# Moving the output combination behind the gating of the next tile on VectorE's queue

## The chip, the cores and the metric

The kernel runs on all 8 cores of one Trainium2 chip, one batch element on each, with the same program and no exchange between them. The metric is the device time of the slowest core, in microseconds (us). Each core has TensorE (matmuls), VectorE, ScalarE, GpSimd, and SyncE, whose queue issues most of the DMAs here. Each engine takes its instructions in the order in which they were written for it.

## What is computed

The reference, cut to what matters, for one batch element of 4096 tokens and width 2048:

```python
xn = _layernorm(x)                                   # per token
q = elu(xn @ Wqk + bqk)                              # q and k are the same
v = silu(xn @ Wv + bv);  u = silu(xn @ Wu + bu)
kv  = einsum('bhnd,bhne->bhde', k, v)                # 16 heads of 128
out = einsum('bhnd,bhde->bhne', q, kv)
out = _layernorm(out, ln_g, ln_b)                    # over all 2048
s   = (u * out) @ Wo + bo
g   = silu(mixture_of_experts(xn))                   # 8 experts, the best 2 of each token
return x + s * g
```

## The kernel before

Everything is built by a `Planner`: `P.step(engine, fn, wait, inc)` appends an instruction (or a small block of them) to the list of that engine, with the semaphore counts that it waits for and that it raises. So the order of the calls in the source is the order of each engine's queue. Each step of VectorE, ScalarE and GpSimd also waits for the step before it on its own engine.

There are three stages with a barrier between them. Stage one makes `xn`, the projections q, v, u and the sum `kv`, and leaves transposed `xn`, transposed q (`qt_s`) and u (`u_s`) in HBM. Stage two is the mixture of experts and leaves its result `y_s` in HBM. Stage three, the one that the change touches, goes over 32 tiles of 128 tokens. A round of its loop (lines 909 to 1008), for tile t:

- SyncE: loads of `qt_t` (two halves, lines 912 and 913; the profile calls the tile `qtt`) and of `u_t` (lines 915, 916), two buffers each.
- TensorE: `att_mms` (line 925), 16 matmuls from `qt_t` and `kv_bf` into `att_ps`, four banks of PSUM.
- GpSimd: `ug_sb` = u times the layernorm gain (line 937), `ub_sb` = u times its offset (line 940).
- ScalarE: two passes over `att_ps` for sum and sum of squares (lines 947, 949), then five short steps to mean and reciprocal deviation (lines 953 to 960).
- VectorE: `n_sb`, the normalised tile (line 964).
- `emit_s_combine(t - 1)`, the projection by Wo and the combination of the tile before (lines 843 to 904). For each of four column blocks dc = 0 to 3: TensorE multiplies `zt_sb` by `wo_sb` into one of two PSUM banks, a bias matmul (line 856) and 16 matmuls (line 860); ScalarE makes silu of `y_t` (line 873); VectorE multiplies the two into `t4_sb` (line 881); GpSimd adds `x_t` into `o_t` (line 889). The matmuls of block dc wait for the VectorE product of the block two before it, which empties their bank. After the fourth block SyncE stores `o_t` (line 896) and loads `x_t` and `y_t` for the next tile (lines 899, 902), both behind the last sum. There is one buffer each of `o_t`, `x_t` and `y_t`.
- VectorE: `t1_sb` = `n_sb` times `ug_sb` (line 972), `z_bf` = `t1_sb` plus `ub_sb` (line 978).
- TensorE transposes `z_bf` in four groups (line 993), and VectorE copies each group to `zt_sb` (line 1002), which the next round's `emit_s_combine` reads.

After the loop, `emit_s_combine(31)` stands alone.

SyncE's queue is in order as well, so the loads of `qt_t` for round t + 1 stand behind the store and the two loads that end `emit_s_combine(t - 1)`. VectorE's order in round t is thus: line 964, four times line 881, line 972, line 978, four times line 1002.

Of the kernel before, what the change touches and what calls it, by code (L numbers as in the profile page):

```python
# [158 lines left out]
def build(upto=None, dbg=False):  # L159
# [69 lines left out]
    P = Planner(nc)  # L229
    for s in ("tE", "vE", "sE", "pE", "bS", "bG", "bV", "bA", "bT"):  # L230
# [10 lines left out]
    w_ready = {0: [  # L241
        P.dma("gpsimd", wsb.rearrange("p (c n) -> p c n", c=KC),
              wd[:, 0:HALF].rearrange("(c p) n -> p c n", p=128))
        for wd, wsb in ((wqk_d, wq_sb), (wv_d, wv_sb), (wu_d, wu_sb))]}
    conv_done = {}
    conv_done["wh1"] = [
        P.dma("gpsimd", wh1_s[i],
# [63 lines left out]
    marks = {"setup": P.mark()}  # L311
# [531 lines left out]
    def emit_s_combine(t):  # L843
        zi = t % 2
        sgw = [ev[("yl", t)]]
        if t > 0:
            sgw.append(("vE", ev[("t4", (t - 1) * 4 + 3)]))
        for dc in range(4):
            pp = dc % 2
            smw = [("vE", ev[("zte", t)]), ev[("wol",)]]  # L850
            prev_dc = t * 4 + dc - 2
            if prev_dc >= 0:
                smw.append(("vE", ev[("t4", prev_dc)]))

            def s_mms(e, dc=dc, pp=pp, zi=zi):
                e.matmul(sps[pp], ones_bf, bo_r[:, dc * 512:(dc + 1) * 512],
                         start=True, stop=False)
                last = None
                for c in range(KC):
                    last = e.matmul(sps[pp], zt_sb[zi][:, c * 128:(c + 1) * 128],  # L860
                                    wo_sb[:, c * D + dc * 512: c * D + (dc + 1) * 512],
                                    start=False, stop=(c == KC - 1))
                return last
            P.step("tensor", s_mms, wait=smw, inc=[("tE", 1)])
            ev[("s_mm", t, dc)] = C["tE"]

            if dc == 0:
                scw = list(sgw)
            elif dc == 1:
                scw = [("vE", ev[("t4", (t - 1) * 4 + 3)])] if t > 0 else []  # L870
            else:
                scw = [("vE", ev[("t4", t * 4 + dc - 2)])]
            P.step("scalar", lambda e, dc=dc: e.activation(
                sg_c[dc % 2], y_t[:, dc * 512:(dc + 1) * 512], AF.Silu),
                wait=scw)
            ev[("sgc", t, dc)] = C["sE"]

            t4w = [("tE", ev[("s_mm", t, dc)]), ("sE", ev[("sgc", t, dc)])]
            if prev_dc >= 0:
                t4w.append(("pE", ev[("comb_c", prev_dc)]))  # L880
            P.step("vector", lambda e, dc=dc, pp=pp: e.tensor_mul(
                t4_sb[:, dc * 512:(dc + 1) * 512], sps[pp], sg_c[dc % 2]),
                wait=t4w, inc=[("vE", 1)])
            ev[("t4", t * 4 + dc)] = C["vE"]

            cbw = [("vE", ev[("t4", t * 4 + dc)]), ev[("xl", t)]]
            if t >= 1 and dc == 0:
                cbw.append(ev[("outs", t - 1)])
            P.step("gpsimd", lambda e, dc=dc: e.tensor_add(  # L889
                o_t[:, dc * 512:(dc + 1) * 512],  # L890
                t4_sb[:, dc * 512:(dc + 1) * 512],
                x_t[:, dc * 512:(dc + 1) * 512]),
                wait=cbw, inc=[("pE", 1)])
            ev[("comb_c", t * 4 + dc)] = C["pE"]
        ev[("comb", t)] = C["pE"]
        ev[("outs", t)] = P.dma("sync", out_d[t * TT:(t + 1) * TT, :], o_t,
                                wait=[("pE", ev[("comb", t)])])
        if t + 1 < NT:
            ev[("xl", t + 1)] = P.dma(
                "sync", x_t, x_d[(t + 1) * TT:(t + 2) * TT, :],  # L900
                wait=[("pE", ev[("comb", t)])])
            ev[("yl", t + 1)] = P.dma(
                "sync", y_t, y_s[(t + 1) * TT:(t + 2) * TT, :],
                wait=[("sE", ev[("sgc", t, 3)]), ev[("ys", (t + 1) // JT)]])
# [4 lines left out]
    for t in range(NT):  # L909
# [56 lines left out]
            wait=[("sE", ev[("l3e", t)])], inc=[("vE", 1)])  # L966
        ev[("nev", t)] = C["vE"]

        if t >= 1:
            emit_s_combine(t - 1)  # L970
            marks[f"p3_comb{t-1}"] = P.mark()
        P.step("vector", lambda e: e.tensor_mul(t1_sb, n_sb, ug_sb),
               wait=[("pE", ev[("ug", t)])], inc=[("vE", 1)])
        ev[("tmul", t)] = C["vE"]
# [5 lines left out]
        ev[("z", t)] = C["vE"]  # L980
        marks[f"p3_t1b{t}"] = P.mark()

        zi = t % 2
        for g4 in range(4):
            zpw = [("vE", ev[("z", t)])]
# [59 lines left out]
```

How the kernel before makes its waits and increments, by code:

```python
            def run(eng):  # L117
                last = {}
                items = self.items[engine]
                if upto is not None:
                    items = items[:upto[engine]]
                for fn, waits, incs in items:
                    for s, v in waits:
                        if last.get(s, 0) >= v:
                            continue
                        eng.wait_ge(self.sems[s], v)
                        last[s] = v
                    inst = fn(eng)
                    for s, a in incs:
                        inst = inst.then_inc(self.sems[s], a)
```

## Time and profile before

| | us |
|---|---|
| median of 3 runs | 10307.86 |
| lowest and highest of them | 10151.63, 11250.75 |
| the profiled execution | 10156.27 |
| its span, slowest core (core 5) | 10154.7 |
| its span, fastest core | 10110.8 |

| engine | busy us | share of the span |
|---|---|---|
| TensorE, matmuls | 7791.6 | 77% |
| VectorE | 2042.0 | 20% |
| ScalarE | 1209.6 | 12% |
| GpSimd | 512.2 | 5% |

The span runs from the first to the last instruction of the slowest core. In the profile PE is TensorE, PEld its weight loads, DVE is VectorE, ACT is ScalarE, POOL is GpSimd, and SPq is the SyncE queue that issues DMAs. L881 is line 881 of the kernel. The granted clock, PEclk, is TensorE's as a share of 2.4 GHz. A row of busy time by stretch gives the stretch (from:to), its length, the busy time with the count of instructions for PE, PEld, DVE, ACT and POOL in this order, the granted clock, the busy share of the DMA engines and their GB/s.

### The profile page before, as it was taken

Reading aid. Unit: us, or ns where it says so; the run is one execution under the profiler, and the core shown is the slowest. Engines: PE = TensorE matmul, PEld = TensorE weight load, DVE = VectorE, ACT = ScalarE, POOL = GpSimd, SP = SyncE. Lnnn points to the kernel's source line nnn. Section 1 sums busy time; section 2 is a strip of 40 time slices with the busy share of each in tenths; the row PEclk is TensorE's granted clock in tenths of the full one; section 3 lists DMA queues with packets and bytes.
Section 4 is the critical chain, followed back from the end, with each engine's and each line's share of the span. In section 5 each row is a group of like instructions: output and inputs, shape, how many; then the busy total and the mean of one; then the engine's idle time right before and its main releaser. Section 6 shows DMA issues by size and latency. Waiting matters only on the chain.

```text
span 10154.7 us, 91183 instructions; the slowest of 8 cores (10110.8 to 10154.7 us)
## 1 busy us (share of the span) xinstructions
PE 7791.6 (77%) x36385; PEld 3503.8 (35%) x36385; DVE 2042.0 (20%) x2716; ACT 1209.6 (12%) x1758; POOL 512.2 (5%) x238
## 2 busy tenths in 40 slices
PE   1001188878887998998998998989989999945555
PEld 0000044433333443443443443434444444422222
DVE  0000033321111221221221221212212212223333
ACT  0000033321111000000000000000000000022222
POOL 0000000000000000000000000000000000024443
PEclk9555588888888999999999999999999999977777
DMA  9999822221112555445445445444454444433223
GB/s 126 109 111 110 101 69 69 70 87 34 34 34 64 154 149 149 149 149 158 149 149 166 149 133 162 148 157 149 148 173 149 149 149 149 141 133 115 108 109 116
DMA packets 1356421, 1251.71 MB, mean 123 GB/s; under 512 B 148426, under 2 KB 1213402, under 8 KB 1332186
## 3 DMA queue, kind: packets, MB, share of 16 engines
q1 hardware_dynamic: 1339764, 1111.65, 34.8%
q0 software_dynamic: 16240, 134.24, 11.9%
q8 instruction: 294, 4.82, 0.2%
q14 instruction: 123, 1.01, 0.0%
HBM read 1262.61 MB, written 239.08 MB: 148 GB/s over the span
## 4 chain that ended last, share of the span: by engine, by line
PE 72%; another core or an unknown queue 11%; DMA 7%; DVE 3%; ACT 3%; issue 2%; SPq 2%; POOL 1%; DVEq 0%; ACTq 0%; POOLq 0%
PE PS L719 18%; PE PS L774 18%; PE PS L724 17%; PE PS L490 10%; PE PS L517 4%; DMA qtt<-qt_s 3%; PE PS L860 3%; DMA xng<-xnt_s 2%; DMA xnt<-xnt_s 2%; SPq L86 1%; PE PS L482 1%; POOL ot L889 1%; DVE nsb L964 1%; ACT nsb L947 1%
## 5 line engine op out<-in xcount | busy, mean ns | idle before, releaser
L719 PE MATMUL PS<-xng,gateb 128*128 128x512 bf16 x8192 | 1868.3, 382 | 208.2 <-DMA xng<-xnt_s 208.2
L774 PE MATMUL PS<-downb,atb 128*128 128x512 bf16 x8192 | 1778.4, 379 | 115.8 <-DVE atb L744 115.8
L724 PE MATMUL PS<-xng,upb 128*128 128x512 bf16 x8192 | 1852.0, 380 | 0.0
L719 PEld LDWEIGHTS PS<-xng,gateb 128*128 128x128 bf16 x8192 | 804.5, 98 | 1189.1 <-issue 233.5
L774 PEld LDWEIGHTS PS<-downb,atb 128*128 128x128 bf16 x8192 | 796.9, 98 | 1097.3 <-issue 145.5
L724 PEld LDWEIGHTS PS<-xng,upb 128*128 128x128 bf16 x8192 | 801.2, 98 | 966.9
L744 DVE TENSOR_TENSOR atb<-sgb,PS 128x512 bf16<-128x512 f32 x512 | 352.3, 688 | 3398.3 <-ACT sgb L738 3398.3
L738 ACT ACTIVATE sgb<-PS 128x512 f32<-128x512 f32 x512 | 305.7, 597 | 5322.4 <-PE PS L724 5322.4
L802 DVE SCALAR_TENSOR_TENSOR yg<-PS,cw_res,yg 128x512 f32<-128x512 f32 x896 | 672.8, 751 | 993.4 <-PE PS L774 945.6
L418 PE MATMUL PS<-id_bf,xnbf 128*128 128x128 bf16 x512 | 36.2, 228 | 989.2 <-DVE xnbf L398 989.2
L490 PE MATMUL PS<-wq,xnt 128*128 128x512 bf16 x2048 | 681.6, 418 | 0.0
L490 PE MATMUL PS<-wvs,xnt 128*128 128x512 bf16 x2048 | 670.7, 412 | 0.0
L937 POOL TENSOR_TENSOR ugsb<-ut,g_rep 128x2048 f32<-128x2048 bf16 x32 | 133.0, 4158 | 8404.3 <-DMA ut<-u_s 8399.8
L860 PE MATMUL PS<-wosb,ztsb 128*128 128x512 bf16 x2048 | 524.9, 416 | 0.0
L517 PE MATMUL PS<-wus,xnt 128*128 128x512 bf16 x2048 | 453.2, 380 | 0.0
L418 PEld LDWEIGHTS PS<-id_bf,xnbf 128*128 128x128 bf16 x512 | 33.2, 102 | 997.0 <-issue 990.2
L490 PEld LDWEIGHTS PS<-wvs,xnt 128*128 128x128 bf16 x2048 | 215.0, 105 | 295.7 <-issue 92.4
L525 DVE TENSOR_SCALAR elm<-PS 128x1024 f32<-128x1024 f32 x64 | 78.4, 1225 | 1131.9 <-PE PS L490 736.0
L860 PEld LDWEIGHTS PS<-wosb,ztsb 128*128 128x128 bf16 x2048 | 204.7, 105 | 293.2 <-issue 117.3
L517 PEld LDWEIGHTS PS<-wus,xnt 128*128 128x128 bf16 x2048 | 195.0, 98 | 253.9 <-issue 27.2
L490 PEld LDWEIGHTS PS<-wq,xnt 128*128 128x128 bf16 x2048 | 171.4, 103 | 255.5 <-issue 109.8
L925 PE MATMUL PS<-kv_bf,qtt 128*128 128x128 bf16 x512 | 59.7, 310 | 252.1 <-DMA qtt<-qt_s 252.1
(117 smaller groups left out, 3017.8 us busy)
## 6 DMA issues: line engine op xcount, KB each, us to landing
gateb<-gbf SPq DMA_DIRECT2D x256, 1024.0 KB, 6.5
upb<-ubf SPq DMA_DIRECT2D x256, 1024.0 KB, 9.6
downb<-dbf SPq DMA_DIRECT2D x64, 4096.0 KB, 18.8
x<-x SPq DMA_DIRECT2D x32, 1024.0 KB, 7.2
gbf<-gw POOLq DMA_DIRECT2D x8, 4096.0 KB, 233.2
ubf<-uw POOLq DMA_DIRECT2D x8, 4096.0 KB, 232.7
dbf<-dw POOLq DMA_DIRECT2D x8, 4096.0 KB, 233.2
y_s<-yg SPq DMA_DIRECT2D x8, 4096.0 KB, 13.8
```

What stands on the lines that cost most here:

```text
L86: self.step(engine, lambda e: e.dma_start(out=out, in_=in_, **kw), wait=wait, inc=[(lane, 16)], _dma=True)
L482: e.matmul(ps_t[:, s2 * 512:(s2 + 1) * 512], ones_bf, br[:, h * HALF + s2 * 512: h * HALF + (s2 + 1) * 512], start=True, stop=False)
L490: last = e.matmul(ps_t[:, s2 * 512:(s2 + 1) * 512], lhs, wsb[:, c * HALF + s2 * 512: c * HALF + (s2 + 1) * 512], start=False, stop=(c == K ...
L517: last = e.matmul(u_ps[:, s2 * 512:(s2 + 1) * 512], lhs, wu_sb[:, c * HALF + s2 * 512: c * HALF + (s2 + 1) * 512], start=False, stop=(c == ...
L719: last = e.matmul(gps[pp], gate_b[qbi][:, c * 256 + fo: c * 256 + fo + 128], xng[:, c * GT:(c + 1) * GT], start=(c == 0), stop=(c == KC - 1))
L724: last = e.matmul(ups[pp], up_b[qbi][:, c * 256 + fo: c * 256 + fo + 128], xng[:, c * GT:(c + 1) * GT], start=(c == 0), stop=(c == KC - 1))
L738: P.step("scalar", lambda e, pp=pp: e.activation(sg_b, gps[pp], AF.Silu), wait=s2w, inc=[("sE", 1)])
L744: P.step("vector", lambda e, fc=fc, pp=pp: e.tensor_mul(at_b[:, fc * GT:(fc + 1) * GT], sg_b, ups[pp]), wait=atw, inc=[("vE", 1)])
L774: last = e.matmul(yp2[pp][:, q * 512:(q + 1) * 512], lhs, down_b[dbi][:, fcc * D + dc * 512: fcc * D + (dc + 1) * 512], start=(fcc == 0), ...
L802: e.scalar_tensor_tensor(ysl, yp2[pp][:, q * 512:(q + 1) * 512], cw_col, ysl, ALU.mult, ALU.add),
L860: last = e.matmul(sps[pp], zt_sb[zi][:, c * 128:(c + 1) * 128], wo_sb[:, c * D + dc * 512: c * D + (dc + 1) * 512], start=False, stop=(c = ...
L937: P.step("gpsimd", lambda e, bi=bi: e.tensor_mul(ug_sb, u_t[bi], g_rep), wait=ugw)
```

## The change

`emit_s_combine(t - 1)` moves from before lines 972 and 978 to behind them. A dictionary `w_slab`, which nothing reads, is added. The call stays ahead of the transposes, so the lists of TensorE, ScalarE, GpSimd and SyncE keep their order. On VectorE the order in round t becomes: line 964, line 972, line 978, four times line 881, four times line 1002.

```diff
+    w_slab = {(nm, si): w_ready[0][j] for j, nm in enumerate(("q", "v", "u"))
+              for si in range(4)}
@@ -966,9 +968,6 @@
             wait=[("sE", ev[("l3e", t)])], inc=[("vE", 1)])
         ev[("nev", t)] = C["vE"]
 
-        if t >= 1:
-            emit_s_combine(t - 1)
-            marks[f"p3_comb{t-1}"] = P.mark()
         P.step("vector", lambda e: e.tensor_mul(t1_sb, n_sb, ug_sb),
                wait=[("pE", ev[("ug", t)])], inc=[("vE", 1)])
         ev[("tmul", t)] = C["vE"]
@@ -980,6 +979,9 @@
         ev[("z", t)] = C["vE"]
         marks[f"p3_t1b{t}"] = P.mark()
 
+        if t >= 1:
+            emit_s_combine(t - 1)
+            marks[f"p3_comb{t-1}"] = P.mark()
         zi = t % 2
         for g4 in range(4):
             zpw = [("vE", ev[("z", t)])]
```

## Rows read from the trace of the kernel before

**Rows 1.** The page, its fourth part: the chain that ended last, by engine

```profile
PE 72%; another core or an unknown queue 11%; DMA 7%; DVE 3%; ACT 3%; issue 2%; SPq 2%; POOL 1%; DVEq 0%; ACTq 0%; POOLq 0%
```

**Rows 2.** Busy time by stretch: stage three from round 1 to round 31

```profile
8985.30:10100.40 1115.10, 650.28 (x3003) 296.05 (x3002) 370.70 (x332) 307.99 (x449) 456.27 (x180) 0.75 0.30 113
```

**Rows 3.** Timeline of one round: start, duration, engine, line, count, [idle before <-releaser]

```profile
9362.85 4.09 POOL L940 TENSOR_TENSOR ubsb<-ut,b_rep 128x2048 f32<-128x2048 bf16 x1
...
9366.49 2.41 DVE L964 TENSOR_SCALAR nsb<-PS,sm 128x2048 f32<-128x2048 f32 x1 [15.30 <-ACT sm L960]
...
9369.00 1.49 DVE L881 TENSOR_TENSOR t4sb<-PS,sgc 128x512 f32<-128x512 f32 x2
...
9374.98 1.26 POOL L889 TENSOR_TENSOR ot<-t4sb,xt 128x512 f32<-128x512 f32 x1 [2.28 <-DVE t4sb L881]
9377.96 0.69 DVE L881 TENSOR_TENSOR t4sb<-PS,sgc 128x512 f32<-128x512 f32 x1 [3.18 <-PE PS L860]
9378.76 2.29 DVE L972 TENSOR_TENSOR t1sb<-nsb,ugsb 128x2048 f32<-128x2048 f32 x1
9378.86 3.31 POOL L889 TENSOR_TENSOR ot<-t4sb,xt 128x512 f32<-128x512 f32 x1 [2.61 <-DVE t4sb L881]
9381.15 3.16 DVE L978 TENSOR_TENSOR zbf<-t1sb,ubsb 128x2048 bf16<-128x2048 f32 x1
...
9383.27 0.82 SPq L86 DMA_DIRECT2D yt<-y_s  x1
...
9384.46 1.01 PE L993 MATMUL PS<-id_bf,zbf 128*128 128x128 bf16 x8 [6.81 <-DVE zbf L978]
...
9386.56 0.95 DVE L1002 COPY ztsb<-PS 128x512 bf16<-128x512 bf16 x2 [0.38 <-PE PS L993]
...
9393.64 1.86 PE L925 MATMUL PS<-kv_bf,qtt 128*128 128x128 bf16 x16 [6.73 <-DMA qtt<-qt_s]
```

**Rows 4.** Timeline of the stage's start: line 978 of tile 0 beside line 937

```profile
8980.63 2.29 DVE L978 TENSOR_TENSOR zbf<-t1sb,ubsb 128x2048 bf16<-128x2048 f32 x1
8980.73 6.14 POOL L937 TENSOR_TENSOR ugsb<-ut,g_rep 128x2048 f32<-128x2048 bf16 x1 [4.54 <-DVE t1sb L972]
...
8985.16 0.95 DVE L1002 COPY ztsb<-PS 128x512 bf16<-128x512 bf16 x2 [0.38 <-PE PS L993]
```

**Rows 5.** Busy time by stretch, of two rounds, cut at TensorE's groups

```profile
9357.19:9358.99 1.80, 1.80 (x17) 1.60 (x17) 0.00 (x0) 0.00 (x0) 0.37 (x1) 0.50 0.32 121
...
9368.60:9369.84 1.24, 0.00 (x0) 0.03 (x1) 1.03 (x3) 0.44 (x1) 0.00 (x0) 1.00 0.00 0
...
9377.70:9384.46 6.76, 0.00 (x0) 0.03 (x1) 6.15 (x3) 0.00 (x0) 3.31 (x1) 0.65 0.23 93
...
9069.30:9071.58 2.28, 0.00 (x0) 0.03 (x1) 2.07 (x3) 1.37 (x3) 0.00 (x0) 1.00 0.00 0
9071.58:9077.13 5.55, 5.55 (x17) 1.98 (x17) 0.65 (x1) 1.26 (x2) 2.54 (x2) 0.69 0.00 0
```

**Rows 6.** Busy time by stretch: first block (30, shortest, longest, sum), third block (31, sum)

```profile
9060.73:9065.32 4.59, 4.59 (x18) 1.70 (x18) 0.00 (x0) 4.13 (x5) 4.45 (x2) 0.83 0.01 4
...
9804.99:9811.19 6.20, 6.20 (x18) 2.11 (x18) 0.00 (x0) 5.58 (x7) 6.06 (x2) 0.61 0.00 0
...
sum 161.91, PE 161.91 PEld 56.98 DVE 0.00 ACT 143.72 POOL 157.60; mean PE 5.40 PEld 1.90 DVE 0.00 ACT 4.79 POOL 5.25
...
sum 139.98, PE 139.94 PEld 52.97 DVE 20.21 ACT 39.06 POOL 78.64; mean PE 4.51 PEld 1.71 DVE 0.65 ACT 1.26 POOL 2.54
```

**Rows 7.** Timeline of the last round and what follows it

```profile
10121.17 0.69 DVE L881 TENSOR_TENSOR t4sb<-PS,sgc 128x512 f32<-128x512 f32 x1 [3.18 <-PE PS L860]
...
10126.48 0.81 SPq L86 DMA_DIRECT2D yt<-y_s  x1
...
10135.31 1.35 ACT L873 ACTIVATE sgc<-yt 128x512 f32<-128x512 f32 x2 [20.83 <-DMA yt<-y_s]
...
10140.14 0.39 PE L856 MATMUL PS<-bo_r,ones_bf 1*128 1x512 bf16 x1
```

## The prediction

> **What bounds the kernel now.** I read the page first. TensorE carries 72% of the chain that ended last [rows 1], yet the span is an average over stages, and the change touches one of them. So I cut the last stage out of it [rows 2]: from its second round on it is 1115.1 us long, with TensorE busy for 650 us, GpSimd 456, VectorE 371, ScalarE 308. No engine is full there; the stage is a loop of waits. Its 30 full rounds (from the `att_mms` of t = 1 at 8985.3 to that of t = 31 at 10100.4) last 1115.1 / 30 = 37.17 us each. Whatever the change does, it does 31 times in this loop and nowhere else.
>
> One round, in order of time, is [rows 3], from 9357.19 (`att_mms` of round t, the first stretch in [rows 5]) to 9393.64 (that of t + 1). I write dc0 to dc3 for the four groups of matmuls of `emit_s_combine(t - 1)`, each begun by its bias matmul of line 856, and t4_0 to t4_3 and comb_0 to comb_3 for the VectorE products (line 881) and GpSimd sums (line 889) behind them. Read down:
> - dc0 and dc1 run while ScalarE does the statistics. VectorE's normalisation (line 964) ends at 9368.90, t4_0 follows at once, and dc2 can start only when t4_0 has emptied its PSUM bank: at 9369.84, after a wait of 1.24 us (the row from 9368.60 in [rows 5]).
> - dc2 and dc3 follow, t4_3 at 9377.96, comb_3 at 9378.86. Here VectorE takes up line 972, and comb_3 lasts 3.31 us against the 1.26 us of the sum at 9374.98, which is the same work.
> - The end of comb_3 (9382.17) lets the SyncE queue issue, in its order, the store of `ot`, the loads of `xt` and `yt`, and behind them the two loads of `qtt`. `att_mms` starts at 9393.64, 11.47 us after comb_3 ended. TensorE's transposes and VectorE's last copy were over at 9387.51; it waits for the DMA (last row of [rows 3]).
>
> So the loop is: att, statistics, line 964, t4_0, dc2, dc3, t4_3, comb_3, SyncE queue, `qtt`, att. Lines 972 and 978, the transposes and the four copies hang beside it. They run in the shadow of comb_3 and of the loads, and only the contention of line 972 with comb_3 reaches the loop.
>
> **The change part by part.** The dictionary `w_slab` is read by nobody: nothing. The move of `emit_s_combine(t - 1)` behind line 978 changes no queue but VectorE's. Line 972 and 978 issue nothing on TensorE, ScalarE, GpSimd or SyncE, so those four queues, DMAs included, keep their order. On VectorE the order becomes 964, 972, 978, t4_0 to t4_3, copies. Queued behind lines 972 and 978 now is t4_0, and dc2 waits for it, and with dc2 the whole tail of the loop.
>
> 1. The two instructions ahead of t4_0. Line 972 takes 2.29 us beside 0.10 us of hand-over. What they read from GpSimd is ready: `ubsb`, the later one, ends at 9366.94, 2.06 us before line 972 could start at 9369.00. Line 978 takes 3.17 us in the loop, but there it shares its start with comb_3. In the first round, with the same operands, it took 2.29 us (first row of [rows 4]); there it started 0.10 us ahead of GpSimd's instruction. In the new place GpSimd is idle. I take 2.29: 2 x 2.29 + 2 x 0.10 = +4.78 us, and 3.17 as the bound above (+0.88). Below 4.78 nothing can go, as both must run.
>
> 2. comb_3 is relieved. Behind t4_3 VectorE now has only the copies. What do they cost GpSimd? Line 937 in [rows 4] took 6.14 us against the 4.09 of its like on line 940 [rows 3]. It had line 978 running beside it for 2.19 us (8980.73 to 8982.92) and four copies, 0.95 us a pair, wholly inside it (the last pair is shown). The excess, 2.05 us, is covered by line 978, and the copies added nothing. So comb_3 returns to 1.26: -2.05 us. Bound: nothing gained, if the copies block it after all. The Trainium skill (SBUF — State Buffer, Who interferes with whom) says that a copy can enter a mode that takes the port pair shared with GpSimd for the whole instruction, while an instruction with at most one SBUF input outside that mode doesn't contend. If all four copies of 0.43 us held comb_3 up, 1.7 us of the 2.05 would be lost; the row speaks for the second half of the rule.
>
> 3. The clock of dc2. TensorE's wait between dc1 and dc2 grows from 1.24 us to 1.24 + 4.78 = 6.0 us in the round shown. In another round a wait of 2.28 us was already followed by a granted clock of 0.69 in dc2, which then lasted 5.55 us instead of 3.86 [rows 5]: the clock went to 1.2 GHz and came back to 2.4 within the group. Over all 31 rounds dc2 takes 139.98 us [rows 6]; without the last (3.86) that is 4.54 us a round, so 12 of 30 rounds pay 1.69. After the longer waits I see the clock low: `att_mms`, which waited for 6.7 us (last row of [rows 3]), runs at 0.50 (the row from 9357.19 in [rows 5]), and from there the clock rises somewhere in dc0. The 30 dc0 groups take 161.91 us together, 5.40 each, the shortest 4.59, the longest 6.20 [rows 6]. At half rate a group loses half of the time that it spends there, so the rise comes 1.80 + 2 x (5.40 - 3.86) = 4.88 us after `att_mms` began (3.26 to 6.48). The same from the start of dc2 gives 3.86 + 4.88 / 2 = 6.30 us; bounds 5.55 (the row seen) and 3.86 + 6.48 / 2 = 7.10. So +6.30 - 4.54 = +1.76 us (+1.01 to +2.56). dc3 then runs at 2.4 GHz as now. The Trainium skill (TensorE: Matmul & The Clock Gate, Why this matters for your kernels) warns of waits between bursts of matmuls for this reason, which speaks against the change; the trace agrees with its 5.55 against 3.86.
>
> 4. What gets earlier and gains nothing. The transposes no longer wait for line 978 (6.8 us of idle before them) but follow dc3 directly, and the copies end some 4 us sooner after t4_3. The next reader is dc0 of the next round, which stands behind `att_mms`, which waits for `qtt`: cover 6.1 us (9387.51 to 9393.64) already. `nsb` and `ugsb` come free earlier too, but ScalarE waits for `att_mms` and GpSimd for `ut`. If that cover were gone, the copies' end would set the loop (last rival).
>
> Sum for a round: 4.78 - 2.05 + 1.76 = +4.49 us; 30 rounds: +135 us.
>
> 5. The last round has no loads of `qtt` behind it. There t4_3 of t = 30 starts 4.78 + (6.30 - 3.86) = 7.22 us later. Behind it the transposes and copies are through about 3 us after t4_3 instead of 9.5, so dc0 and dc1 of the last combination end about 11 us after it, and then the load of `yt` is late next: comb_3 ends 2.16 after t4_3, the issue follows 1.10 later, `yt` is used 8.83 after that [rows 7], one ScalarE product (0.67) and t4_0 (0.84 to the start of dc2) follow, so dc2 starts 13.7 us after t4_3, against 18.97 now (10121.17 to 10140.14). TensorE waits about 3 us before it, so I add 1.3 for the clock. Net +7.22 - 5.3 + 1.3 = +3 us.
>
> Total: +138 us. The profiled span is 10154.7, the execution's time 10156.27. 10156.3 + 138 = 10294 us, 1.4% more. That execution lies at the lower end of the runs shown (10151.63 to 11250.75, median 10307.86); the prediction stands against 10156, not against that median.
>
> **The rivals.**
> A. *The clock costs nothing new* (the longer wait falls as often into a low stretch as before): 4.78 - 2.05 = 2.73 x 30 = 82 us, 10239. Against it: the 2.28 us of [rows 5] already brought the clock down, and the waits of 6.8 and 6.7 us in the round shown end at 0.50.
> B. *comb_3 isn't relieved*, because the copies hold GpSimd as line 972 does: 4.49 + 2.05 = 6.54 x 30 = 196, with the tail 10355. Against: the 6.14 us row.
> C. *The clock stays low through dc2 and dc3*: 2 x 3.86 - 0.68 = 7.04 in place of 1.76, 9.77 x 30 = 293, with the tail about 10454, 2.9% slower. It needs a rise later than 7.7 us after a burst's start; the latest of 30 is 6.48.
> D. *Not slower*: the chain over line 978, transposes and copies sets the round, and not `qtt`. Then the 6.76 us before the transposes [rows 5] vanish against 4.78 + 1.76 added: -0.2 a round, 10150. It decides where `qtt` lands before the copies end; the trace has it 6.1 us after. For over 2% faster, 6.8 us a round would have to go, with 4.78 put in; I see no row for that.
>
> **How the numbers follow.** Forecast 0.72; A 0.06, B 0.07, C 0.09, D 0.06. The forecast's own range is 30 x (4.78 - 2.05 + 1.01) = 112 to 30 x (4.78 + 0.88 - 2.05 + 2.56) = 185, so 10270 to 10345. With A and B the range is 10230 to 10375. Over 2% (about what a measurement of this kernel can tell from no change) begins at 10359: C and a part of B with the upper bounds, 0.12. Faster by over 2%: 0.02. Within 2%: 0.86.
>
> **What would show it.** Step 1: line 978 at 2.29 in all rounds and dc2 starting 17.4 us after `att_mms` instead of 12.65. Step 2: the longest `ot` sum at about 1.3. Step 3: dc2 mean near 6.3, dc3 3.9; granted clock 0.6 to 0.7 in dc2 in each round. Step 4: transposes right behind dc3, `att_mms` still waiting for `qtt`, now 11.5 us after comb_3. Rounds of 41.7 us; stages before unchanged. It is wrong if `qtt` isn't what `att_mms` waits for, or if the clock behaves otherwise after the longer wait.

## The result

| | before | after |
|---|---|---|
| median | 10165.26 us (10 runs) | 10618.93 us (10 runs) |
| lowest | 10147.57 | 10274.16 |
| span of core 5 in the profiled execution | 10154.7 | 10232.7 |
| mean round of stage three, core 5 | 37.17 | 40.99 |

Eight of the ten timed executions of the changed kernel and three of the ten of the kernel before were more than 1.5% above the lowest of their kernel, and in those eight at least one die (four cores) had a mean granted clock of 0.78 to 0.86 instead of 0.88. The executions that are left give a ratio of 1.0173, with a 95% interval of 1.0104 to 1.0242; of the changed kernel these are only two, 10274.16 and 10399.68 us, and in the second all eight cores had a clock of 0.865 to 0.868. The ratio of the two lowest times is 1.0125. The rows below are of core 5, whose granted clock was never between its two levels in either profile. In `after` the line numbers of stage three are 2 higher than before, except for the two moved-ahead instructions, which are lines 971 and 977.

Busy time by stretch of the changed kernel, the answer to [rows 2] and [rows 5]: the stage from round 1 to round 31; then, of one round, the end of dc1 with TensorE's wait ahead of dc2 behind it, dc2, and dc3. The columns are those of [rows 2].

```profile
8947.15:10176.93 1229.78, 648.81 (x3003) 287.39 (x3001) 344.55 (x332) 308.01 (x449) 394.84 (x180) 0.75 0.27 103
9449.00:9457.30 8.30, 1.53 (x8) 0.51 (x6) 7.71 (x5) 2.54 (x3) 0.54 (x1) 0.81 0.00 0
9457.32:9462.90 5.58, 5.58 (x18) 1.94 (x18) 0.65 (x1) 1.26 (x2) 2.53 (x2) 0.68 0.01 1
9462.90:9466.75 3.85, 3.85 (x20) 1.74 (x20) 0.69 (x1) 0.00 (x0) 1.26 (x1) 1.00 0.00 0
```

The 30 rounds take 1229.8 us instead of 1115.1, with TensorE as busy as before: 114.7 us more of waiting. The span of core 5 grew by only 78 us, because the first `att_mms` of the stage already started at 8928.4 us instead of 8966.6; on the other cores of the kernel before it started between 8926 and 8950, so core 5 was the latest of the eight there. GpSimd is busy for 61 us less (394.84 against 456.27) and VectorE for 26 us less (344.55 against 370.70). The second row's clock of 0.81 is a mean over a stretch that begins at 1.00 and ends at 0.50.

The timeline of the same round of the changed kernel, against [rows 3]:

```profile
9439.92 1.87 PE L927 MATMUL PS<-kv_bf,qtt 128*128 128x128 bf16 x16 [11.60 <-DMA qtt<-qt_s]
...
9449.17 2.41 DVE L966 TENSOR_SCALAR nsb<-PS,sm 128x2048 f32<-128x2048 f32 x1 [20.25 <-ACT sm L962]
...
9451.69 2.29 DVE L971 TENSOR_TENSOR t1sb<-nsb,ugsb 128x2048 f32<-128x2048 f32 x1
9454.08 2.29 DVE L977 TENSOR_TENSOR zbf<-t1sb,ubsb 128x2048 bf16<-128x2048 f32 x1
9456.48 1.49 DVE L883 TENSOR_TENSOR t4sb<-PS,sgc 128x512 f32<-128x512 f32 x2
9457.32 0.58 PE L858 MATMUL PS<-bo_r,ones_bf 1*128 1x512 bf16 x1 [6.78 <-DVE t4sb L883]
...
9467.16 0.69 DVE L883 TENSOR_TENSOR t4sb<-PS,sgc 128x512 f32<-128x512 f32 x1 [3.18 <-PE PS L995]
9467.95 0.95 DVE L1004 COPY ztsb<-PS 128x512 bf16<-128x512 bf16 x2
9468.05 1.26 POOL L891 TENSOR_TENSOR ot<-t4sb,xt 128x512 f32<-128x512 f32 x1 [2.61 <-DVE t4sb L883]
...
9480.66 1.87 PE L927 MATMUL PS<-kv_bf,qtt 128*128 128x128 bf16 x16 [11.23 <-DMA qtt<-qt_s]
```

Most of the mechanism can be read here. Lines 971 and 977 take 2.29 us each and stand ahead of t4_0; dc2 starts 17.40 us after `att_mms` (12.65 before), after TensorE waited 6.78 us for it. comb_3 takes 1.26 us instead of 3.31, with two copies running beside it. `att_mms` still waits for `qtt`, now for 11.2 us instead of 6.7, and starts 11.35 us after comb_3's end (9469.31), as before (11.47): what the transposes win is idle time.

Busy time by stretch, cut like [rows 6]: the shortest and the sum of the 30 dc2 groups of the changed kernel.

```profile
10112.99:10118.42 5.43, 5.43 (x18) 1.89 (x18) 0.65 (x1) 1.26 (x2) 2.53 (x2) 0.70 0.00 0
...
sum 172.39, PE 172.38 PEld 59.17 DVE 19.46 ACT 37.77 POOL 75.95; mean PE 5.75 PEld 1.97 DVE 0.65 ACT 1.26 POOL 2.53
```

dc2 averages 5.75 us; before it was 4.54, with 18 groups at 3.86 and 12 at 5.55. No group is at the 3.86 of the high clock any more. The wait and the length of dc2 go against each other: after a wait of 6.07 us dc2 took 6.29, after one of 6.75 us it took 5.61. In 25 of the 30 rounds the two together make 12.36 or 12.37 us.

### The profile page after: what moved, and what is told of

It is laid out like the page before. It is cut to its first block, busy times and chain, and to the rows that moved or that the text cites. A ratio compares the mean times of both kernels' runs of the same rounds, so it can differ in the third digit from the quotient of the medians.

```text
span 10552.1 us, 91063 instructions; the slowest of 8 cores (10232.7 to 10552.1 us)
## 1 busy us (share of the span) xinstructions
PE 8118.6 (77%) x36385; PEld 3582.1 (34%) x36385; DVE 2015.0 (19%) x2716; ACT 1209.8 (11%) x1758; POOL 448.7 (4%) x238
## 3 DMA queue, kind: packets, MB, share of 16 engines
q0 software_dynamic: 16240, 134.24, 11.4%
q14 instruction: 123, 1.01, 0.0%
## 4 chain that ended last, share of the span: by engine, by line
PE 73%; another core or an unknown queue 10%; DMA 6%; DVE 4%; ACT 3%; issue 2%; SPq 1%; POOL 0%; DVEq 0%; ACTq 0%; POOLq 0%
PE PS L721 17%; PE PS L776 17%; PE PS L726 17%; PE PS L492 11%; PE PS L519 5%; PE PS L862 3%; DMA qtt<-qt_s 2%; DMA xnt<-xnt_s 2%; DMA xng<-xnt_s 1%; SPq L86 1%; PE PS L484 1%; DVE nsb L966 1%; DVE zbf L977 1%; DVE t1sb L971 1%
## 5 line engine op out<-in xcount | busy, mean ns | idle before, releaser
L492 PE MATMUL PS<-wvs,xnt 128*128 128x512 bf16 x2048 | 770.8, 466 | 0.0
L492 PE MATMUL PS<-wq,xnt 128*128 128x512 bf16 x2048 | 770.7, 466 | 0.0
L519 PE MATMUL PS<-wus,xnt 128*128 128x512 bf16 x2048 | 548.9, 436 | 0.0
L862 PE MATMUL PS<-wosb,ztsb 128*128 128x512 bf16 x2048 | 547.4, 428 | 0.0
L492 PEld LDWEIGHTS PS<-wvs,xnt 128*128 128x128 bf16 x2048 | 237.3, 116 | 358.1 <-issue 355.3
L519 PEld LDWEIGHTS PS<-wus,xnt 128*128 128x128 bf16 x2048 | 216.2, 108 | 328.3 <-issue 328.3
```

Source lines behind the costliest of these rows:

```text
L492: last = e.matmul(ps_t[:, s2 * 512:(s2 + 1) * 512], lhs, wsb[:, c * HALF + s2 * 512: c * HALF + (s2 + 1) * 512], start=False, stop=(c == K ...
L519: last = e.matmul(u_ps[:, s2 * 512:(s2 + 1) * 512], lhs, wu_sb[:, c * HALF + s2 * 512: c * HALF + (s2 + 1) * 512], start=False, stop=(c == ...
```

## The experiments

The theory is the loop of the prediction: `att_mms`, statistics, line 964, t4_0, dc2, dc3, t4_3, comb_3, SyncE queue, `qtt`. Rounds and dc2 below are means over the 30 rounds of one core: core 5, in `fill` and `early_split_y2_fill` core 1. The granted clock of these cores in these rounds was 0.50 or 1.00, except in `early_before`, where 5 of the 30 rounds had 0.81 (without them the means are 31.54 and 5.83).

| kernel | round, us | dc2, us |
|---|---|---|
| before | 37.17 | 4.54 |
| after | 40.99 | 5.75 |
| `after_again` | 41.08 | 5.78 |
| `mul_ahead` | 40.27 | 5.40 |
| `mul_twice` | 43.92 | 6.55 |
| `fill` | 39.23 | 3.86 |
| `split` | 34.67 | 4.09 |
| `early_before` | 31.48 | 5.64 |
| `early_after` | 29.15 | 6.12 |
| `early_split` | 26.69 | 6.32 |
| `early_split_y2` | 23.85 | 5.55 |
| `early_split_y2_fill` | 22.21 | 3.86 |

One core isn't the whole chip. Core 5 had the longest round of the kernel before, together with core 0 (the eight cores: 36.86 to 37.17, mean 37.04) and the shortest of `split` (34.67 to 35.40, mean 35.03); in `after_again` the eight lie at 40.97 to 41.21, mean 41.09. By these means the change costs 4.05 us a round, and `split` gains 2.0.

The lowest device times that aren't named below are 10369.27 us (`mul_twice`) and 10226.44 (`mul_ahead`), against 10126.38 for the kernel before on that chip; 10213.81 (`early_before`), 9889.84 (`early_after`) and 10077.87 (`early_split`), against 10127.27; and 10024.77 (`early_split_y2`), against 10211.74. No execution of `early_before`, `early_split` and `early_split_y2` had a mean clock of 0.88 or more on both dies, so their rounds say more than these times.

### The change once more

> The changed kernel once more, on one chip with the kernel before. Theory (the round of stage three is a loop through the qtt loads; the change adds 4.78 us of VectorE ahead of dc2, takes 2.05 us off the last GpSimd sum, and makes dc2 longer by the clock): rounds of 41.0 us against 37.2, stages one and two as before, 115 to 130 us more in all, a ratio of 1.012. Rival (the change also lengthens the stages ahead of it, as the median of 10619 us could suggest): stages one and two are longer in this kernel than in the one before on cores whose granted clock is the same, and the ratio is 1.02 or more.

Measured: rounds of 41.08 us. The lowest time was 10253.13 us against 10126.38 of the kernel before on the same chip, +127 us (1.3%). The medians there were 10915.86 (8 runs) and 10357.75 (11 runs), and in the two later comparisons, on two other chips, the kernel before alone had medians of 11175.84 and 11090.88 (11 runs each). In the profiled execution `att_mms` of the first round starts at 8936.9 us on core 5, against 8966.6 in the kernel before: the stages ahead aren't longer. The rival falls. With the mean of all cores, 4.05 us a round, the loop accounts for 122 of the 127 us. What made the first profile of the changed kernel longer on other cores can be seen in the busy time of one stretch of stage one, first core 3 and then core 5:

```profile
2600.00:2610.00 10.00, 8.60 (x45) 3.96 (x42) 3.28 (x4) 5.46 (x5) 0.00 (x0) 0.81 0.04 17
...
2600.00:2610.00 10.00, 9.16 (x48) 4.01 (x46) 4.27 (x4) 5.67 (x5) 0.00 (x0) 1.00 0.00 1
```

The granted clock is 0.81 against 1.00, in matmuls that the change doesn't touch, thousands of microseconds ahead of stage three. The Trainium skill (TensorE: Matmul & The Clock Gate, Part 1: The HAM clock gate) describes a peak-current limit of 13/16 of the clock, which would be this 0.81, once three cores of a die run dense matmuls; the level agrees, the condition no run here shows, because the times of each core count from its own start.

### Is the end of comb_3 in the loop?

The product is made a second time behind the t4 products:

```diff
         if t >= 1:
             emit_s_combine(t - 1)
             marks[f"p3_comb{t-1}"] = P.mark()
+        P.step("vector", lambda e: e.tensor_mul(t1_sb, n_sb, ug_sb), inc=[("vE", 1)])
+        ev[("tmul", t)] = C["vE"]
```

> The changed kernel with the product of line 971 made a second time, behind the four t4 products, so that it runs beside the last GpSimd sum as in the kernel before. It does this work twice and the output is the same. Theory: the last sum takes 3.3 us again, and the loop carries it: round 41.0 + 2.05 = 43.0 us, 62 us above the changed kernel. Rival (the length of the last sum does not reach the loop, the loads have slack): round 41.0, no difference.

```profile
9160.58 2.29 DVE L985 TENSOR_TENSOR t1sb<-nsb,ugsb 128x2048 f32<-128x2048 f32 x1
9160.68 3.31 POOL L891 TENSOR_TENSOR ot<-t4sb,xt 128x512 f32<-128x512 f32 x1 [2.61 <-DVE t4sb L883]
```

(Timeline of this kernel, core 5, at comb_3.) The sum takes 3.31 us again, and the round is 43.92, 2.93 us above the changed kernel and 0.9 above the 43.0 expected: 2.05 from comb_3 as expected, and 0.80 from dc2, which now takes 6.55 us although nothing was changed between `att_mms` and dc2. `att_mms` still waits for `qtt`, 10.9 us on average. So the 2.05 us are in the loop, and the mean length of dc2 depends on something besides the wait ahead of it (6.3 us on average, 6.7 in the changed kernel). The rival falls.

### Half of the move

`emit_s_combine(t - 1)` stands between lines 971 and 977 of the changed kernel, so that only the product is ahead of it:

```diff
         ev[("tmul", t)] = C["vE"]
+        if t >= 1:
+            emit_s_combine(t - 1)
         zw = []
```

> Half of the move: the product (line 972 of before) ahead of the combination, the sum that makes z (line 978) behind it as in the kernel before. Theory: dc2 starts 2.39 us later than before, at 15.05 us; the sum for z now stands beside the last GpSimd sum and holds it at about 3.3 us, so nothing is won there; dc2 waits 3.5 us or more and finds the clock low in most rounds, about 5.6 us instead of 4.54. Round 37.17 + 2.39 + 1.1 = 40.6 us, almost the whole loss of the full change. Rival (no contention term, each instruction moved ahead costs only its length): round near 39.0, half of the loss.

Measured, as means of the 30 rounds: dc2 starts 14.97 us after `att_mms`, comb_3 takes 3.24 us, dc2 5.40, the round 40.27. Half of the move makes 3.1 of the 3.8 us. Worked out: 2.32 for the start of dc2 and 0.86 for its length give 3.18, and almost nothing comes back. The rival, with its 39.0, falls: the cost isn't proportional to what is moved ahead. The first half pays 0.86 of the 1.21 us for the clock, and the second gets the 2.05 us of comb_3.

### The clock of dc2

24 matmuls in TensorE's wait, ahead of dc2:

```diff
+            if dc == 2 and t + 1 < NT:
+                def warm(e, zi=zi):
+                    last = None
+                    for _k in range(24):
+                        last = e.matmul(PS[:, 3584:4096], zt_sb[zi][:, 0:128],
+                                        wo_sb[:, 0:512], start=True, stop=True)
+                    return last
+                P.step("tensor", warm, wait=[("vE", ev[("zte", t)])], inc=[("tE", 1)])
             P.step("tensor", s_mms, wait=smw, inc=[("tE", 1)])
```

> The changed kernel with 24 matmuls of 128x512 ahead of dc2, into a PSUM bank that nobody reads, which keep TensorE busy for about 5.2 of the 6.6 us that it waits. They add work and change no result. Theory: the clock is still at 2.4 GHz when dc2 starts, dc2 takes 3.87 instead of 5.75 us, round 41.0 - 1.9 = 39.1 us, 57 us less than the changed kernel. Rival (dc2 is long for another reason than the wait, such as its weight loads): dc2 stays at 5.75 and the round at 41.

```profile
8983.03 5.34 PE L870 MATMUL PS<-wosb,ztsb 128*128 128x512 bf16 x24
...
8990.10 0.37 PE L858 MATMUL PS<-bo_r,ones_bf 1*128 1x512 bf16 x1 [1.73 <-DVE t4sb L891]
```

(Timeline of this kernel, core 1.) The wait that is left is 1.73 us, dc2 starts where it did, and takes 3.86 us in all 30 rounds; the round is 39.23, 1.76 below the changed kernel's 40.99, against the 1.89 that dc2 gave back. Work that nobody needs makes the loop faster, because it stands where TensorE idled. The rival falls, and the clock term of the change is confirmed by itself. A gain in the time of the whole kernel isn't shown: the lowest of its six times is 10337.22 us, against 10253.13 of the changed kernel on another chip. In the profiled execution the cores 0 to 3, 6 and 7 had rounds of 39.17 to 39.38 us, but the cores 4 and 5 had a granted clock of 0.81 in 24 of the 30 rounds, and means of 41.50 and 41.33.

### The relief alone

The product goes behind t4_1 and the sum for z behind t4_2, where VectorE waits for dc2 and dc3:

```diff
-        P.step("vector", lambda e: e.tensor_mul(t1_sb, n_sb, ug_sb), ...)
-        P.step("vector", lambda e: e.tensor_add(z_bf, t1_sb, ub_sb), ...)
         if t >= 1:
-            emit_s_combine(t - 1)
+            emit_s_combine(t - 1, {1: emit_mul, 2: emit_add})
...
             ev[("t4", t * 4 + dc)] = C["vE"]
+            if dc in behind:
+                behind[dc]()
```

> The product behind the second t4 product and the sum for z behind the third, both in VectorE's waits for dc2 and dc3. Theory: dc2 starts at 12.65 us as in the kernel before, the last GpSimd sum finds VectorE without a two-input instruction and takes 1.27 us, round 37.17 - 2.05 = 35.1 us, 60 us less than before, and the transposes follow dc3 directly. Rival (GpSimd's first sums or VectorE's products are delayed by the contention moved there): t4_3 starts later than 20.8 us after att_mms and the round stays near 37.

```profile
9032.90 4.55 POOL L893 TENSOR_TENSOR ot<-t4sb,xt 128x512 f32<-128x512 f32 x2 [3.14 <-DVE t4sb L883]
9033.47 2.85 DVE L974 TENSOR_TENSOR t1sb<-nsb,ugsb 128x2048 f32<-128x2048 f32 x1
...
9037.75 2.29 DVE L982 TENSOR_TENSOR zbf<-t1sb,ubsb 128x2048 bf16<-128x2048 f32 x1
9037.85 3.31 POOL L893 TENSOR_TENSOR ot<-t4sb,xt 128x512 f32<-128x512 f32 x1 [0.41 <-DVE t4sb L883]
...
9041.73 1.27 POOL L893 TENSOR_TENSOR ot<-t4sb,xt 128x512 f32<-128x512 f32 x1 [0.56 <-DVE t4sb L883]
```

(Timeline of this kernel, core 5.) The contention is still there, 2.85 us for the product, 4.55 for the first two sums and 3.31 for the third, but the engines had idle time at these places, and comb_3 takes 1.27. The round is 34.67, 2.50 below before: 2.05 for comb_3 and 0.45 for dc2 (4.09). The lowest time is 10072.72 against 10126.38, -54 us, with -60 expected. The rival falls: on core 5 t4_3 starts 21.0 us after `att_mms` on average, against 21.4 before, and no core has a mean round over 35.40 us.

### Why the round hung on `qtt`

The loads of `qt_t` and `u_t` for round t + 1 are issued in round t, ahead of the store and loads that wait for comb_3:

```diff
     for t in range(NT):
         bi = t % 2
-        (loads of qt_t and u_t for t)
+        if t == 0:
+            load_qu(0)
+        if t + 1 < NT:
+            load_qu(t + 1)
```

> The kernel before with the loads of qtt and ut for round t + 1 issued in round t, one round earlier in the SyncE queue. Theory: att_mms no longer waits for qtt but follows the transposes; the round ends at the transposes' end, about 30.4 us instead of 37.2, 200 us less. Rival (the DMA queue or the loads of yt set the round): the wait turns into one of ScalarE for yt and the round stays above 35.

> The changed kernel with the same early loads. Theory: with qtt out of the loop the round ends at the transposes in both orders; the 4.78 us and the longer dc2 are now paid back by the transposes that no longer wait for the sum for z: round about 29.8 us, within 1 us of the other order with early loads. So the change costs time only because the round hangs on qtt. Rival (the longer VectorE chain costs its 3.8 us in any case): round 3.8 us above that of the kernel before with early loads.

Measured: 31.48 us for the order of before, 29.15 for that of after. In both `att_mms` follows the transposes without a wait for `qtt` (timelines on core 5, first `early_before`, then `early_after`):

```profile
9464.49 1.92 PE L932 MATMUL PS<-kv_bf,qtt 128*128 128x128 bf16 x16
...
9444.17 1.05 PE L934 MATMUL PS<-kv_bf,qtt 128*128 128x128 bf16 x16
```

My 30.4 for the first was too low: with no idle time ahead of `att_mms` dc0 is shorter (4.36 instead of 5.32), the wait ahead of dc2 is longer and dc2 takes 5.64. But the sign of the change has turned: the same move costs 3.8 us a round while `qtt` ends the loop, and saves 2.3 us once it doesn't. The forecast of no more than 1 us between them was missed on the side of more gain. Both rivals fall: the round of `early_before` isn't above 35, and the later VectorE chain doesn't cost its 3.8 us in any case.

The split order with the early loads:

> The split order with the early loads. Theory: dc2 starts at 12.65 us, the transposes follow dc3 at 20.4 and att_mms follows them at 23.3 us; the loads of yt for the next tile land about 9 us into the next round, before ScalarE wants them at 10.5. Round about 23.5 us, 410 us less than before (ratio 0.96). Rival: the loads, which now have to come every 23.5 us, or the single buffer of yt set the round, at 27 us or more.

```profile
9075.79 1.28 ACT L875 ACT_TABLE_LOAD   x1 [3.54 <-DMA yt<-y_s]
9077.08 1.35 ACT L875 ACTIVATE sgc<-yt 128x512 f32<-128x512 f32 x2
9077.95 1.49 DVE L883 TENSOR_TENSOR t4sb<-PS,sgc 128x512 f32<-128x512 f32 x2 [3.12 <-ACT sgc L875]
9078.79 0.58 PE L858 MATMUL PS<-bo_r,ones_bf 1*128 1x512 bf16 x1 [6.05 <-DVE t4sb L883]
```

(Timeline of this kernel, core 5.) The round is 26.69, not 23.5. I had the landing of `yt` before ScalarE's need; it landed behind it, ScalarE waited 3.54 us for it and VectorE 3.12 us for ScalarE, and dc2 took 6.32 us on average. The rival with the single buffer was right in kind, though it had 27 us or more. Two buffers of `yt`, loaded a round earlier:

```diff
-    y_t = arena.alloc("yt0", [128, D], F32)
-    t1_sb = arena.alloc("t1sb", [128, D], F32)
+    y_b = [arena.alloc(f"yt{i}", [128, D], F32) for i in range(2)]
...
+        if t + 2 < NT:
+            ev[("yl", t + 2)] = P.dma(
+                "sync", y_b[zi], y_s[(t + 2) * TT:(t + 3) * TT, :],
```

> The split order with early loads, and two buffers of yt, loaded one round earlier (the product is written over nsb to make room). Theory: in the kernel with one buffer t4_0 started at 12.3 to 14.0 us instead of 11.0 because ScalarE waited for yt; with two it starts at 11.0, dc2 at 11.9, takes about 5.5 us after a wait of 3 us at a low clock, and the round is 11.9 + 5.5 + 6.4 = 23.8 us instead of 26.7, 2.9 us less a round, some 9700 us in all. Rival (the loads all together are the limit, four megabytes a round): the round stays near 26.7 and another load is waited for.

> The same with 12 matmuls ahead of dc2 into a PSUM bank that nobody reads. They add work and change no result. Theory: dc2 comes at 2.4 GHz, 3.87 us instead of 5.5, round 1.6 us shorter, about 22.2 us. Rival: the clock rises or falls with what goes before the short wait as well, and dc2 stays above 5 us.

Measured: 23.85 us with dc2 at 5.55, and with 12 matmuls in the wait 22.21 us with dc2 at 3.86, both as the theory had it, so both rivals fall. In the last kernel the cores 4 and 5 had a granted clock of 0.81 in part of the rounds, and means of 23.63 and 23.71; the other six lie at 22.17 to 22.21. The last kernel's lowest time is 9749.27 us, against 10211.74 for the kernel before on that chip, which is 462 us less (and 377 less than the lowest time of before on any chip, 10126.38); the rounds on core 1 give 30 x (37.17 - 22.21) = 449.

## Why the prediction was right or wrong

**Right, and by its own steps.** The chain through `qtt`, read from [rows 3], carries the difference in stage three: 40.99 - 37.17 = 3.82 us a round, 115 us in 30 rounds. Step 1, +4.78 us: dc2 starts 4.75 us later and line 977 takes 2.29. Step 2, -2.05 us: comb_3 at 1.26, and `mul_twice` puts the 2.05 back. Step 4: the transposes follow dc3 and `att_mms` starts 11.4 us behind comb_3, when `qtt` has landed. Step 5: the part of the span behind the last `att_mms` started at 10176.93 and took 55.8 us against 54.3, so +1.5 beyond what the rounds had added; I had +3.

**Mis-sized: step 3.** The longer dc2 costs 5.75 - 4.54 = 1.21 us, not 1.76 (it lies inside the +1.01 to +2.56 given). The step took the time from the start of `att_mms` to the clock's rise, averaged over rounds of 37 us, and counted it from the start of dc2, as if the rise kept its distance from the start of the group. It doesn't: dc2 is shorter after a longer wait, and in 25 of 30 rounds the clock came back so that dc2 ended 12.4 us after dc1 had, whether the wait was 6.07 or 6.94 us long. Nor can the 4.88 us be carried from one kernel to another: in the changed kernel dc0 too is shorter, 4.98 on average instead of 5.32 over the same 30 rounds (the 5.40 of [rows 6] leaves out the first of them and has the one after the last). And `mul_twice`, with a wait ahead of dc2 that is no longer (6.3 us on average against 6.7) and a round 3 us longer, has a dc2 of 6.55 (5.37 to 7.03). What sets the point in the round at which the clock rises is left open; `mul_twice` shows only that it isn't what stands between `att_mms` and dc2 alone. By the means of eight cores, 5.76 in `after_again` and 4.34 before, the term is 1.42 us, so a part of the miss on core 5 is that core's own 4.54. On core 5 the 0.55 us make 17 of the 20 us between 135 and 115; the other 0.1 us a round lie in the start of dc2 (4.75 for 4.78) and in small differences of when `qtt` lands, which I haven't taken apart.

**Wrong: what the number was set against.** The ten timed executions had a median of 10618.93 us, outside the range of 10230 to 10375. The step that failed is the base of the total, 10156.3, with the sentence that the prediction "stands against 10156, not against that median", and with it "stages before unchanged": it put at nothing what a granted clock below 1.00 does ahead of the loop and in it. The three times shown, 10151.63, 10307.86 and 11250.75, already said that an execution can be 150 or 1100 us longer, and no rival and no part of the range priced that. What stood in its place can be read in the changed kernel's first profile: on core 1, whose granted clock was 0.81 in parts of stage two and in nearly all of stage three, the first `att_mms` started at 9150 us against 8928 on core 5, the rounds were 42.62 us against 40.99, and the span was 10506.0 against 10232.7. Of these 273 us the forecast had none. Whether the change itself makes such executions more frequent (eight of ten against three of ten here, six of eight against six of eleven beside `after_again`) isn't shown; two later chips had ten of eleven of them with the kernel before alone, so they don't need the change. On the lowest times the change was worth +127 us twice (10253.13 against 10126.38, and 10274.16 against 10147.57), with +138 forecast; the ratio of 1.0173 (1.0104 to 1.0242) holds the forecast's 1.014, with the two executions behind it that the result names.

**The rivals.** A (no clock cost) and C (low clock through dc3) fall by the rows of dc2 and dc3, B by comb_3's 1.26. D's condition, `qtt` landing before the copies end, doesn't hold in the kernel; where it was made to hold, the change became a gain, more than D gave it.

## What to carry to other kernels

Before an instruction is moved ahead on an in-order queue, find what ends the loop: the move costs its full length if the instruction behind it is on that chain, and what it releases early is worth nothing if that release has slack. The same move cost 3.8 us a round with the loads late and gained 2.3 with them early, so mend the order of the loads first. And look for the idle stretch of the engine: the same two instructions, placed where VectorE waited for TensorE anyway, gained 2.5 us a round on core 5 and 2.0 on the mean of the cores.

## What the runs showed of the hardware that I had not expected

- Whether a short wait of TensorE brings the clock down isn't told by its length alone: in the kernel before, waits of 1.74 and 1.99 us ahead of dc2 were followed by a low stretch (dc2 5.55 us) and waits of 1.88 and 1.92 us weren't (3.86), and in `mul_ahead` six waits of 3.08 to 3.14 us weren't either. Matmuls that nobody needs, put into a wait, shortened the round by 1.8 us on a core that never had the 0.81 of the last point.
- Once the clock is down, a longer wait isn't a longer loss: in the changed kernel the wait and dc2 together made 12.36 or 12.37 us in 25 of 30 rounds. But the loss differs between loops: after waits of some 6.7 us dc2 was 1.9 us longer than at the high clock in rounds of 41 us, and after waits of some 6.3 us 2.7 us longer in rounds of 44 us. Whether the length of the loop or the order in it does that isn't shown.
- The granted clock has a third level in the records, 0.81. In the changed kernel's first profile the cores 2 and 3 had it from about 1244 to 3773 us (the later half of stage one and the start of stage two), the cores 0 and 1 from 8131 us on, through nearly all of stage three, and the cores 4 to 7 never; in the kernel before no core had it. On the first four cores it made spans of 10506 to 10552 us against 10233 to 10266 on the others, more than the change did. Why it comes in pairs of cores and at different places of their execution is open.
